# The values of two key blocks in one step of TensorE, with three slots of exponentials, in a two-layer transformer kernel

## The reference, cut to what matters

```python
Q = Q * cos + _rotate_half(Q) * sin          # layer 0, K likewise
scores = jnp.einsum('bhqd,bhkd->bhqk', Q, K) / scale
scores = jnp.where(causal, scores, jnp.float32(-jnp.inf))
attn = jax.nn.softmax(scores, axis=-1)
out = jnp.einsum('bhqk,bhkd->bhqd', attn, V) # @ Wo.T + bo
```

## Time and profile before

| | us |
|---|---|
| runs | 1579.21, 1581.62, 1581.71 (median 1581.62) |
| the profiled execution | 1581.71 |
| its span, first to last instruction | 1580.0 |
| TensorE busy | 1498.6 (95%) |
| VectorE busy | 1138.0 (72%) |
| ScalarE busy | 853.8 (54%) |
| granted TensorE clock, mean | 0.977 of full speed |

### The profile page before, as it was taken

One profiled execution on the slowest core, in us unless ns is written; L12 is line 12 of the kernel. 1 busy time (PEld: TensorE's weight loads), 2 busy tenths in 40 slices (PEclk: granted clock), 3 DMA queues, 4 the chain that ended last, 5 costly groups with the idle time before them and its releaser, 6 DMA issues.

```text
span 1580.0 us, 26931 instructions
## 1 busy us (share of the span) xinstructions
PE 1498.6 (95%) x10398; PEld 794.9 (50%) x10398; DVE 1138.0 (72%) x2546; ACT 853.8 (54%) x1661; POOL 239.0 (15%) x196
## 2 busy tenths in 40 slices
PE   4599999999999999999999999999999999999998
PEld 3345445564546544554445644556444554446444
DVE  7788887777675677567887768877776677785851
ACT  1115545556665755666355445454756576664674
POOL 6211202002011302013020021110302131201000
PEclk9779999999999999999999989999999999999999
DMA  5114030030304022230400502004021300304000
GB/s 181 40 41 82 2 81 2 2 81 2 81 2 81 2 43 41 50 85 1 81 2 2 134 1 64 19 1 81 2 48 36 77 6 2 82 2 107 3 2 27
DMA packets 44094, 66.27 MB, mean 42 GB/s; under 512 B 7328, under 2 KB 18880, under 8 KB 43968
## 3 DMA queue, kind: packets, MB, share of 16 engines
q1 hardware_dynamic: 40800, 63.77, 18.1%
q10 hardware_dynamic: 3168, 0.79, 0.2%
HBM read 9.23 MB, written 4.19 MB: 8 GB/s over the span
## 4 chain that ended last, share of the span: by engine, by line
PE 85%; DVE 7%; ACT 4%; issue 2%; POOL 1%; DMA 0%; ACTq 0%; DVEq 0%; POOLq 0%
PE WB L1033 25%; PE O L1178 18%; PE WB L1133 16%; PE ST L1158 15%; PE ST L1161 3%; PE WB L1136 3%; ACT PT L739 3%; PE WB L1186 2%; DVE mxa L971 1%; DVE rope_b L871 1%; PE WB L1194 1%; PE WB L1058 1%; PE WB L1099 1%; DVE veps L825 1%; DVE mxb L971 1%
## 5 line engine op out<-in xcount | busy, mean ns | idle before, releaser
L739 ACT ACTIVATE PT<-ST 128x512 f32<-128x512 f32 (+1 forms) x1216 | 634.5, 578 | 394.0 <-PE ST L1161 292.1
L971 DVE TENSOR_REDUCE mxa<-WB 128x1 f32<-128x512 f32 (+3 forms) x864 | 531.6, 664 | 145.7 <-PE WB L1136 97.3
L1133 PE MATMUL WB<-KS,QS 96*128 96x512 bf16 (+3 forms) x1536 | 436.2, 332 | 7.3 <-DVE attn L1005 4.3
L1158 PE MATMUL ST<-QS,KS 99*128 99x512 bf16 (+3 forms) x1536 | 429.4, 329 | 12.1 <-ACT PT L739 9.7
L1178 PE MATMUL O<-PT,Vaug 128*17 128x512 f32 (+3 forms) x3072 | 323.0, 494 | 7.2 <-ACT PT L739 4.3
L1158 PEld LDWEIGHTS ST<-QS,KS 99*128 99x128 bf16 x1536 | 144.2, 98 | 210.4 <-ACT PT L739 118.9
L971 DVE TENSOR_REDUCE mxb<-WB 128x1 f32<-128x384 f32 (+3 forms) x352 | 213.6, 635 | 36.9 <-PE WB L1136 36.1
L1133 PEld LDWEIGHTS WB<-KS,QS 96*128 96x128 bf16 x1536 | 146.0, 99 | 186.4 <-DVE mxa L971 55.3
L1136 PE MATMUL WB<-negmask,identb 128*128 128x128 bf16 x1024 | 199.8, 222 | 0.0
L1161 PE MATMUL ST<-negmaskT,identb 128*128 128x128 bf16 x1024 | 197.5, 220 | 0.0
L608 POOL TENSOR_TENSOR proj<-proj,parts 128x512 f32<-128x512 f32 x64 | 74.1, 1161 | 457.5 <-ACT parts L699 457.4
(11 more groups left out here) (139 smaller groups left out, 1351.9 us busy)
## 6 DMA issues: line engine op xcount, KB each, us to landing
QS<-parts SPq DMA_DIRECT2D x96, 256.0 KB, 5.0
KS<-parts SPq DMA_DIRECT2D x96, 256.0 KB, 5.0
x<-in_x SPq DMA_DIRECT2D x4, 1024.0 KB, 5.6
out<-x SPq DMA_DIRECT2D x8, 512.0 KB, 2.9
QS<-nmT ACTq DMA_DIRECT2D x32, 24.0 KB
w_q<-in_w_q SPq DMA_DIRECT2D x2, 256.0 KB, 6.1
w_k<-in_w_k SPq DMA_DIRECT2D x2, 256.0 KB, 6.0
cos<-in_cos SPq DMA_DIRECT2D x1, 512.0 KB, 5.5
```

The source lines that it names most:

```text
L739: act.activation(PT[:, q % PT_SLOTS, j:j + n, 0:wd], src, ACT.Exp, scale=float(SCALE[STAGES[k][1]])).then_inc(exp_done.sem, 1)
L971: dve.tensor_reduce(dst, bank, AX.X, ALU.max).then_inc(emptied, 1)
L1133: mm = pe.matmul(bank[:, q * wd:(q + 1) * wd], QS[0:KR, h + qb * P:h + (qb + 1) * P], KS[0:KR, h + seg * BANK:h + seg * BANK + wd], start= ...
L1158: mm = pe.matmul(ST[:, o + i * wd:o + (i + 1) * wd], KS[0:KM, h + kb * P:h + (kb + 1) * P], QS[0:KM, h + q0:h + q0 + wd], start=True, stop ...
```

## The change

`weighted_values` becomes a step for two key blocks: it waits once, for the last exponential of the second block, and then issues the eight products one after the other; `pv_done` is still raised after each block. The planner has 6 such jobs a group in place of 12, each with a cost of 250 ns and the columns of both blocks (before: 246 ns and the columns of one). `PT` gets a third slot. In the plan the exponentials of a block wait for the whole step that holds the block three before (`| 1`), in the program for that block alone. The room comes from `attnT`, which is now a view of `xn`; `normalise` gets a wait for the product by Wo two stages back.

```diff
-W_BANKS, ST_BANKS, PT_SLOTS = 4, 3, 2
+W_BANKS, ST_BANKS, PT_SLOTS = 4, 3, 3
...
+            if old >= 0:
+                prev = prev + [("dve", ("wo", old, 3))]
...
-                    free = [("pe", ("pv", o // NPV // NG, o // NPV % NG, o % NPV))] if o >= 0 else []
+                    free = [("pe", ("pv", o // NPV // NG, o // NPV % NG, o % NPV | 1))] if o >= 0 else []
...
-            for v, (half, kb) in enumerate(PVS):
+            for v in range(1, NPV, 2):
+                half, kb = PVS[v]
                 due = gs + tg * PV_LAST[v] / NEX - 500
-                cols = BANK - max(kb - 4 * half, 0) * P
+                cost = 250 + sum(4 * (BANK - max(j - 4 * half, 0) * P) / 2.4 for j in (kb - 1, kb))
...
-                job("pe", ("pv", k, g, v), mm(cols, 4) + 230, due, [("act", ("exp", k, g, PV_LAST[v]))] + free
+                job("pe", ("pv", k, g, v), cost, due, [("act", ("exp", k, g, PV_LAST[v]))] + free
...
-        attnT = sb("attnT", [P, 2, KC, 2 * P])
+        attnT = xn[:, :, :, :].rearrange("p i n (c t) -> p i (n c t)", c=KC).rearrange("p i (c t) -> p i c t", c=KC)
...
+                    if k >= 2:
+                        dve.wait_ge(*full(("wo", k - 2, i + 2)))
...
-            def weighted_values(k, g, v):
-                half, kb = PVS[v]
-                pe.wait_ge(*exp_done.upto(k, g * NEX + PV_LAST[v] + 1))
-                if kb == 0:
+            def weighted_values(k, g, last):
+                half = PVS[last][0]
+                pe.wait_ge(*exp_done.upto(k, g * NEX + PV_LAST[last] + 1))
+                if PVS[last][1] == 1:
...
+                for v in (last - 1, last):
+                    kb = PVS[v][1]
+                    slot = ((k * NG + g) * NPV + v) % PT_SLOTS
+                    cols = BANK - max(kb - 4 * half, 0) * P
+                    for j in range(GH):
+                        h = g * GH + j
+                        mm = pe.matmul(O[32 * j:32 * j + VA, BANK - cols:BANK], Vaug[:, kb, h * VA:(h + 1) * VA],
+                                       PT[:, slot, j, 0:cols], start=(kb == 0), stop=(kb == 4 * half + 3), tile_position=(0, 32 * j))
+                    mm.then_inc(pv_done.sem, 1)
```

More of the change, by code:

```diff
@@ L240, in plan @@
                     o = (k * NG + g) * NPV + v - PT_SLOTS
-                    free = [("pe", ("pv", o // NPV // NG, o // NPV % NG, o % NPV))] if o >= 0 else []
+                    free = [("pe", ("pv", o // NPV // NG, o // NPV % NG, o % NPV | 1))] if o >= 0 else []
                 free += [("act", ("exp", o // NEX // NG, o // NEX % NG, o % NEX)) for o in last_u]
                 job("act", ("exp", k, g, u), ac(n * w), due, [("pe", ("st", k, g, u))] + free)
-            for v, (half, kb) in enumerate(PVS):
+            for v in range(1, NPV, 2):
+                half, kb = PVS[v]
                 due = gs + tg * PV_LAST[v] / NEX - 500
-                cols = BANK - max(kb - 4 * half, 0) * P
+                cost = 250 + sum(4 * (BANK - max(j - 4 * half, 0) * P) / 2.4 for j in (kb - 1, kb))
                 free = []
-                if kb == 0 and m + half >= 1:
+                if kb == 1 and m + half >= 1:
                     o = m + half - 1
                     free = [("act", ("ocopy", o // 2 // NG, o // 2 % NG, o % 2))]
-                if k or g or v:
-                    o = (k * NG + g) * NPV + v - 1
+                if k or g or v > 1:
+                    o = (k * NG + g) * NPV + v - 2
                     free.append(("pe", ("pv", o // NPV // NG, o // NPV % NG, o % NPV)))
-                job("pe", ("pv", k, g, v), mm(cols, 4) + 230, due, [("act", ("exp", k, g, PV_LAST[v]))] + free
-                    + ([(emptier(("v", k)), ("v", k, i)) for i in range(4)] if g == 0 and v == 0 else []), PE_LAG)
+                job("pe", ("pv", k, g, v), cost, due, [("act", ("exp", k, g, PV_LAST[v]))] + free
+                    + ([(emptier(("v", k)), ("v", k, i)) for i in range(4)] if g == 0 and v == 1 else []), PE_LAG)
             for t in range(2):
@@ L1171, in weighted_values @@
                         pe.wait_ge(o_zero, 1)
-                if g == 0 and v == 0:
+                if g == 0 and last == 1:
                     pe.wait_ge(*empty(("v", k, 3)))
[L1174 to L1180, removed]
+                for v in (last - 1, last):
[7 more added lines that the diff above has]
+                    mm.then_inc(pv_done.sem, 1)
             def turn_outputs(k, g, t):
```

## The result

The changed kernel takes 1557.5 us (1556.3 to 1558.9, 4 runs), the one before 1581.4 beside it: a ratio of 0.985, interval 0.984 to 0.987. The forecast was 1554 us. The profiled execution took 1556.3 us with a span of 1554.6.

What follows compares the result with a forecast made beforehand. TensorE, busy 95% of the span, was taken as the bound. 1581.7 - 42 (turns) + 9 (exponentials) + 1 (third slot) + 3 (VectorE) = 1553 us, stated as 1554; range 1541 to 1573.

Steps and rivals of the forecast that it cites:

- The turn: TensorE's switch to the values step and back: each joined one saves 0.23 us, 184 fewer give -42 us.
- ScalarE becomes the bound: Rival: exponentials late in most groups, so pairs lose 0.25 us at 60 to 100% of places; about 1600 us; 7%.
- a block pays and not a turn: Rival: each block pays 0.24 us for its own first weights, so joining saves nothing; 1582 to 1590 us; 4%.
- the half-eaten case: Rival: a third of the pairs lose 0.25 us instead of winning 0.23; 1571 us, 1565 to 1578 around it; 20%.
- Waits for exponentials: TensorE waits as each pair needs two blocks' exponentials: +9 us, from a low end of +6 to a high end of +20.
- place 2: Spot with next to no work between values steps: a pair's period 5.35 us against 5.10 before, losing 0.25.
- place 3: Spot with 4.0 us of TensorE work between pairs, ScalarE also needing 4.0: no wait, the whole 0.23 us won.
- The third slot: Second block's exponentials wait for the pair's first block, at most 0.35 us a pair where ScalarE is late: +1 us.
- VectorE: TensorE asks sooner for `WB` banks that VectorE must empty: +3 us, low end 0, high end 10.
- The clock: TensorE's half clock after long waits, 1.7 us lost each time: 0 in the sum, kept as a rival.
- a sign that I had named for being wrong: Windows at half clock appearing between 200 and 600 us would show the forecast wrong.
- the rival: More low clock: longer waits before pairs bring six more half-clock stretches at 1.7 us, +10, 1564 us; 9%.

Runs made afterwards that it cites:

- e3: Changed kernel, same lists and slots, but 164 of the 192 pairs split around the step ahead: 1586.0 us, 1.005 to the kernel before.
- e2: Changed kernel with two slots of exponentials in place of three, planned anew: 1584.0 us, 1.002 to the kernel before.
- e1: Changed kernel with the joining undone, each block its own step, three slots kept: 1575.6 us, 0.997 to the kernel before.
- e8: Changed kernel with only narrow blocks joined, planned with measured durations of exponentials and maxima: 1557.7 us, 0.987 to the kernel before.
- e5: Changed kernel, all pairs joined, planned with measured durations of exponentials and row maxima: 1577.1 us, 0.999 to the kernel before.

## Why the prediction was right, and where it was off

**The turn.** 0.23 us was taken, 0.238 is the median, and e3 shows it as a cost by itself, in unchanged lists. 184 turns are 43.8 us; -42 was forecast. The pair takes 1.84 us; 1.82 was worked out. The two last rivals, that ScalarE becomes the bound and that a block pays and not a turn, are out, and so is the half-eaten case by its time, though of the 43.8 us 18.5 were given back (waits, clock and rest).

**Waits for exponentials.** +9 was forecast. Of the split's waits, those ahead of scores went from 22.9 to 37.4 us and those ahead of the values step from 11.1 to 7.7: +11. The count along the lists came near in the difference, and in part by luck. Its level was wrong: it gave 20 us before and 26 after, where the starts show 34.0 and 45.1; its 20 agreed with the 20 made from the page's 14, but neither is what the starts show. And the places did not go as worked out: place 2 loses 0.95 us and not 0.25, since ScalarE's queue also issues a DMA there, and place 3, at which nothing was to be waited for, waits some 0.3 us and so wins nothing.

**The third slot.** +1 was forecast for pairs that still wait for a slot; the trace after shows no such wait. That the slot was needed at all was argued, its size wasn't: without it, and with the plan that goes with that, pairs are 26 us slower (e2), and it goes with 4 us without pairs (e1).

**VectorE.** +3 was forecast. The prediction called these waits few, by one row of 6.6 us; counted by starts, the waits ahead of products in `WB` are 72 us before, twice those for exponentials, and two of them for VectorE (21.8 and 10.7 us) make up almost half. They hardly grew: those ahead of maxima and other bf16 products in `WB` went from 16.1 to 20.0, those ahead of f32 products from 56.2 to 55.9: +3.6.

**The clock.** 0 in the sum, +1.7 in the split. But where it would show was wrong. I had put 0 because waits of place 2's kind are under a microsecond. At place 2, behind waits shown as 0.26, 0.42 and 0.56 us, the granted clock is 0.50 for 3.4 us, and the second pair takes 3.14 us in place of 1.84:

```profile
1503.60:1507.00 3.40, 3.40 (x19) 0.72 (x12) 0.00 (x0) 0.59 (x2) 0.00 (x0) 0.50 0.00 0
200.00:600.00 400.00, 391.07 (x2856) 221.71 (x2852) 295.05 (x660) 229.96 (x450) 56.03 (x45) 0.99 0.20 41
800.00:1000.00 200.00, 193.35 (x1362) 107.75 (x1360) 159.91 (x358) 102.99 (x202) 24.40 (x19) 1.00 0.19 44
```

From 200 to 600 us, where the earlier trace rows had 1.00, it is 0.99 now: windows at half clock stand there, from 213.4 and from 349.9 us, a sign that I had named for being wrong. Neither comes behind a wait ahead of a pair. They come behind single long waits that the kernel before doesn't have there, one for VectorE and one for an exponential:

```profile
212.64 3.07 PE L1040 MATMUL WB<-w_u,xT 128*128 128x512 f32 x4 [2.80 <-DVE mxb L978]
...
348.28 0.88 PE L1165 MATMUL ST<-QS,KS 99*128 99x512 bf16 x2 [1.83 <-ACT PT L744]
```

From 800 to 1000 it has risen from 0.97 to 1.00, and the sum is nearly even. So half clock did come to new places, as the rival had it; that it left others and so nearly evened out was not foreseen and is luck. That the waits brought it is read from what stands ahead of it; no run tests it.

**The other signs.** TensorE's busy time fell by 32.3 us, not 35 to 45. The page's waits for exponentials went to 15.9 us, not 18 to 30, and are neither fewer nor longer. By starts they are 45.1, at the mark of 45 that I had set for being wrong, but that mark was set on the page's count.

**The order.** The forecast took the list as given and priced its gaps, and that was right for this list. It hid how much hangs on it: the same six pairs a group took 1557.5, 1566.4, 1570.2 and 1577.1 us with plans that differ in the duration of one or two jobs. The change's own durations are the best of the four, and those are not the ones that the trace shows. Unjoined blocks with three slots went from 1575.6 to 1564.7 us by a plan alone, so against the best unjoined list that was tried all pairs gain 7 us and not 24; for the unjoined blocks with two slots no other plan was tried. Why the list of pairs is so sensitive stays open; the runs only show that it is waits (up to 16 us more) and clock (up to 5.0), and not turns.

## What to carry to other kernels

Where TensorE is the bound, look for what lies between its products: here a switch to a product in column tiles and back cost 0.24 us, putting two such steps one behind the other saved it, and taking only that back made the kernel 27 us slower. Ask at once what the longer step now waits for and give that its buffer, since without the third slot the joined kernel was no faster than the one before. When lists come from a planner, one run of one plan doesn't judge an idea to better than 10 or 20 us in 1560; run it with two or three sets of durations, or in fixed lists as in e3.

## What the hardware showed that I had not expected

The lower clock came behind a row of short waits (0.26, 0.42, 0.56 us) between 512-column scores, and it cost one pair 1.3 us. Counted by starts that stretch was emptier than its row says: from 1498.80 to 1503.15 us the columns of the products take 1.9 of the 4.35 us. Issuing one DMA held ScalarE's queue for 0.76 us, more than one exponential of 512 columns (0.48 from start to start). What the lower clock takes moves with the lists, from 19.4 us in e8 to 32.7 in e5, in kernels with the same products. It doesn't follow the time: the change, as fast as e8, loses 27.7.
